# Sandwich block with expert-choice MoE on one core: ranks of the top-k by prefix scans, index lists for two experts at a time, and a later second gather

## The reference

```python
# E = 16, C = int(T * 2.0 / 16) = 1024, D = 256, I = 1024, IS = 512
logits = flat_x @ gate_w.T
scores = softmax(logits, axis=-1).T               # E x T
topk_weight, topk_idx = top_k(scores, C)          # per expert
xg = flat_x[topk_idx]                             # gather
g = einsum('ecd,eid->eci', xg, Wg);  u = einsum('ecd,eid->eci', xg, Wu)
eo = einsum('eci,edi->ecd', gelu(g) * u, Wd) * topk_weight[..., None]
flat_out = zeros.at[topk_idx].add(eo)             # scatter-add
shared = (gelu(hidden @ Sg.T) * (hidden @ Su.T)) @ Sd.T    # every token
x = x + layernorm(flat_out + shared)
```

## Time and profile before

| what | value |
|---|---|
| median of three runs | 2111.92 us |
| profiled execution, its span | 2114.11 us, 2112.3 us |
| TensorE busy | 2030.2 us (96% of the span) |
| TensorE weight load busy | 1814.4 us (86%) |
| VectorE busy | 1195.0 us (57%) |
| ScalarE busy | 971.2 us (46%) |
| GpSimd busy | 436.1 us (21%) |
| granted TensorE clock, mean | 0.981 |

### The profile page before, as it was taken

How to read it: one execution, slowest core, us unless ns; L and a number is a source line. 1 busy time by engine, 2 the same in 40 slices (tenths; PEclk the granted TensorE clock), 3 DMA queues, 4 the chain that set the end, 5 groups by cost and what they waited for, 6 DMA issues and landing times.

```text
span 2112.3 us, 32697 instructions
## 1 busy us (share of the span) xinstructions
PE 2030.2 (96%) x12590; PEld 1814.4 (86%) x12592; DVE 1195.0 (57%) x2518; ACT 971.2 (46%) x1809; POOL 436.1 (21%) x450
## 2 busy tenths in 40 slices
PE   7999999999994998899999999999999999999996
PEld 6899999999984887788888888888989898888885
DVE  5586686677663876555465545444453535343565
ACT  4464564564542334344444444444443434344543
POOL 0000000000001000313323332333233222322255
PEclk8999999999995999999999999999999999999998
DMA  3011110111015111233333333333333333334266
GB/s 112 1 41 42 61 62 41 60 78 43 32 51 196 66 61 41 63 100 74 71 82 79 73 72 82 80 75 75 79 77 79 77 78 91 62 92 100 53 196 131
DMA packets 55556, 159.91 MB, mean 76 GB/s; under 512 B 9472, under 2 KB 25984, under 8 KB 48256
## 3 DMA queue, kind: packets, MB, share of 16 engines
q1 hardware_dynamic: 28912, 116.16, 15.3%
q0 software_dynamic: 26512, 41.96, 12.5%
HBM read 98.78 MB, written 59.31 MB: 75 GB/s over the span
## 4 chain that ended last, share of the span: by engine, by line
PE 64%; DVE 2%; issue 1%; POOL 1%; ACT 1%; DVEq 0%; another core or an unknown queue 0%; ACTq 0%; POOLq 0%
PE mo_psD L58 7%; PE mo_psD L60 7%; PE mo_psD L59 7%; PE mo_psG L58 7%; PE mo_psU L58 7%; PE mo_psG L59 7%; PE mo_psG L60 7%; PE mo_psU L60 7%; PE mo_psU L59 7%; PE mo_psX L1217 1%; PE mo_psX L1033 1%; DVE mo_st L1509 0%; POOL mo_rs L1799 0%; DVE mo_HF L1545 0%; DVE mo_XT_lo L1485 0%
## 5 line engine op out<-in xcount | busy, mean ns | idle before, releaser
L1545 DVE TENSOR_TENSOR mo_HF<-mo_psU,mo_HF 128x512 f32<-128x512 f32 x320 | 221.2, 691 | 645.7 <-ACT mo_HF L1386 625.1
L1386 ACT ACTIVATE mo_HF<-mo_psG 128x512 f32<-128x512 f32 x320 | 191.2, 598 | 478.4 <-PE mo_psU L60 428.9
L1771 POOL DMA_INDIRECT ACC<-mo_OUT,mo_GI x128 | 202.9, 1585 | 700.4 <-ACT mo_OUT L1453 690.9
L60 PE MATMUL mo_psD<-mo_wd_hi,mo_H_lo 128*128 128x256 f32 x1024 | 289.8, 283 | 0.0
L59 PE MATMUL mo_psD<-mo_wd_lo,mo_H_hi 128*128 128x256 f32 x1024 | 289.8, 283 | 0.0
L58 PE MATMUL mo_psD<-mo_wd_hi,mo_H_hi 128*128 128x256 f32 x1024 | 289.6, 283 | 0.0
L1490 DVE TENSOR_TENSOR mo_H_lo<-mo_HF,mo_H_hi 128x512 fp32r<-128x512 f32 x300 | 204.5, 682 | 0.0
L1364 ACT ACTIVATE mo_H_hi<-mo_HF 128x512 fp32r<-128x512 f32 x320 | 199.7, 624 | 1.0 <-DVE mo_HF L1545 1.0
L59 PEld LDWEIGHTS mo_psD<-mo_wd_lo,mo_H_hi 128*128 128x128 f32 x1024 | 196.5, 192 | 1.3
L58 PEld LDWEIGHTS mo_psD<-mo_wd_hi,mo_H_hi 128*128 128x128 f32 x1024 | 196.5, 192 | 1.2
L60 PEld LDWEIGHTS mo_psD<-mo_wd_hi,mo_H_lo 128*128 128x128 f32 x1024 | 196.5, 192 | 0.0
(11 more groups left out here) (262 smaller groups left out, 5177.1 us busy)
## 6 DMA issues: line engine op xcount, KB each, us to landing
X1a<-wg_in SPq DMA_DIRECT2D x16, 1024.0 KB, 4.9
X1a<-wu_in SPq DMA_DIRECT2D x16, 1024.0 KB, 4.9
X1a<-wd_in SPq DMA_DIRECT2D x16, 1024.0 KB, 4.9
XN<-XNB SPq DMA_DIRECT2D x8, 1088.0 KB, 4.1
X<-x_in SPq DMA_DIRECT2D x8, 1024.0 KB, 6.2
out_dram<-X SPq DMA_DIRECT2D x8, 1024.0 KB, 4.3
XN2T<-xn2T SPq DMA_DIRECT2D x8, 1024.0 KB, 3.8
mo_F<-ACC SPq DMA_DIRECT2D x7, 1024.0 KB, 13.0
```

The lines of the kernel that those rows point to most:

```text
L60: return pe.matmul(out, w_lo, x_hi, start=False, stop=last)
L1386: a.activation(HF[:, it % 2, :], psG[:, it % 2, :], ACT.Gelu).then_inc(s_gelu, 1)
L1545: v.tensor_tensor(HF[:, it % 2, :], psU[:, it % 2, :], HF[:, it % 2, :], ALU.mult).then_inc(s_mul, 1)
L1771: g.indirect_dma_start(out=io["ACC"], out_offset=bass.IndirectOffsetOnAxis(ap=GI[n % 2][:, 4 * tb + t:4 * tb + t + 1], axis=0), in_=OUT[:, ...
```

## The change

Three things change.

First, ranks. The masks stay in the transposed layout. A running count along each partition's 1024 columns (`v_scan`, one for each mask) gives every token's place among its partition's marked ones, and three matmuls of one column (`p_off`) with a 0/1 matrix `before` (same expert, earlier partition) and `same` (same expert) give what the other partitions add. VectorE adds, selects and joins the two (`v_slot`, `v_slot2`), TensorE transposes the 128 x 1024 result back by eight matmuls (`p_slot`), and ScalarE copies it as integers (`a_slot`). The 16 transposes, the 20 counting matmuls, their copies and the prefix sums over tables are gone.

Second, lists. `GROUPS, GE` is 8, 2 in place of 4, 4. A group has two chunks of 64 columns, each column holding 32 positions for 2 experts, and the matmuls of a chunk are 32 of 64 x 64 in place of 16 of 128 x 128. There are still 16 chunks: two stand before the experts, at steps 35 and 36, and fourteen in blocks E0+1 to E0+14. SyncE writes and reads lists eight times, with two writes each, in place of four times with four. The list of experts 2 and 3 is decoded in `down(E0+2)`; before, experts 0 to 3 had theirs in the first list.

Third, `gather(1)` waits until TensorE has finished four steps of block E0.

```diff
-GROUPS, GE = 4, 4
+GROUPS, GE = 8, 2
...
+        if x == 28:
+            self.v_scan(v, self.SG, self.GT)
+        if x == 29:
+            self.v_scan(v, self.SE, self.EQ)
         if x == 29.5:
-            self.v_prefix(v)
-            self.v_ahead(v)
-        if x == 31:
-            self.v_rank(v)
             self.v_slot(v)
+        if x == 30:
+            self.v_slot2(v)
         if x == 32:
-            self.v_slot2(v)
             self.v_digits(v)
-        if x == 33:
+        if x == 33.5:
             self.v_lo1(v, 0)
-        if x == 33.5:
             self.v_hival(v, 0)
         if x == 34:
-            self.v_acc(v, 0)
             self.v_lo1(v, 1)
         if x == 35:
+            self.v_acc(v, 0)
             self.v_hival(v, 1)
         if x == 36:
             self.v_acc(v, 1)
...
             self.v_dec(v, 0)
...
-        if x in (34, 36, 37.5, 39):
-            self.p_list(pe, (34, 36, 37.5, 39).index(x))
+        if x == 29.5:
+            self.p_off(pe)
+        if x == 31:
+            self.p_slot(pe)
+        if x in (35, 36):
+            self.p_list(pe, x - 35)
...
+        if x == 31:
+            self.a_slot(a)
         if x == 33:
             self.a_digits(a)
...
+    def v_scan(self, v, out, mask):
+
+        v.tensor_tensor_scan(out[:, :], mask[:, :], mask[:, :], 0.0, ALU.add, ALU.max).then_inc(self.s_scan, 1)
+
+    def p_off(self, pe):
+
+        pe.wait_ge(self.s_scan, 2)
+        gt, eq = (t[:, SC_N - 1:SC_N] for t in (self.SG, self.SE))
+        pe.matmul(self.ps[:, 0, 0:1], self.before[:, :], gt, start=True, stop=True)
+        pe.matmul(self.ps[:, 0, 1:2], self.before[:, :], eq, start=True, stop=False)
+        pe.matmul(self.ps[:, 0, 1:2], self.same[:, :], gt, start=False, stop=True).then_inc(self.s_off, 1)
+
+    def v_slot(self, v):
+
+        v.wait_ge(self.s_off, 1)
+        v.tensor_scalar(self.OFF[:, :], self.ps[:, 0, 0:2], -4097.0, None, ALU.add)
         v.drain()
+        v.scalar_tensor_tensor(self.SG[:, :], self.SG[:, :], self.OFF[:, 0:1], self.GT[:, :], ALU.add, ALU.mult)
+        v.scalar_tensor_tensor(self.SE[:, :], self.SE[:, :], self.OFF[:, 1:2], self.EQ[:, :], ALU.add, ALU.mult)
         v.drain()
+    def v_slot2(self, v):
+        v.scalar_tensor_tensor(self.SLOT[:, :], self.SG[:, :], 4096.0, self.SE[:, :], ALU.add, ALU.add).then_inc(self.s_slot, 1)
+
+    def p_slot(self, pe):
+        pe.wait_ge(self.s_slot, 1)
+        for t in range(8):
+            i = pe.transpose(self.ps[:, t // 4, t % 4 * P:(t % 4 + 1) * P], self.SLOT[:, t * P:(t + 1) * P], self.c.ident[:, :])
+        i.then_inc(self.s_slt, 1)
...
-            i = pe.matmul(self.ps[:, 0, 0:SL * GE], self.lo1[:, t, :, :].rearrange("p v e -> p (v e)"),
+            i = pe.matmul(self.ps[0:SL * GE, 0, 0:SL * GE], self.lo1[:, t, :, :].rearrange("p v e -> p (v e)"),
                           self.val[:, :, t * GE:(t + 1) * GE], start=(t == 0), stop=(t == tiles - 1))
...
-                if n in (2, 4, 6):
-                    topk.store(sp, n // 2)
+                if 1 <= n < GROUPS:
+                    topk.store(sp, n)
...
                 wait(g, s_tw, n - 1)
+                if n == 1:
+                    wait(g, s_up, base[E0] + 4)
```

More of the change, by code:

```diff
@@ L725, in __init__ @@
         self.hi1, self.val = new("hi1", [P, SL, CW], BF16), new("val", [P, SL, CW], BF16)
-        self.vf = new("vf", [P, GE * SL])
-        self.vu, self.vj, self.vp = (new(n, [P, GE * SL], I32) for n in ("vu", "vj", "vp"))
-        self.LS = new("LS", [P, GROUPS, GE, SL], I32)
+        self.vf = new("vf", [GE * SL, GE * SL])
+        self.vu, self.vj, self.vp = (new(n, [GE * SL, GE * SL], I32) for n in ("vu", "vj", "vp"))
+        self.LS = new("LS", [GE * SL, GROUPS, GE, SL], I32)
         self.zero = mem.over("zero", [P, 4 * D], F32, "lo1", 0)
@@ L841, in pool @@
         g.iota(self.TVi[:, :], [[P * NU, 4], [P, NU], [0, GE]], base=P * P, channel_multiplier=1)
-        g.memset(self.ones[:, :], 1.0)
         for i in range(NBIT + 4):
@@ L901, in v_const @@
         v.tensor_scalar(self.same[:, :], self.mcolf[:, :], self.mrowf[:, 0:1], None, ALU.is_equal)
+        v.drain()
+        v.tensor_tensor(self.before[:, :], self.before[:, :], self.same[:, :], ALU.mult)
         v.wait_ge(self.s_scv, 1)
@@ L906, in v_masks @@
         thr = self.cand[:, 0:1].bitcast(F32)
[L907 to L931, removed]
-            i = pe.matmul(self.ps[:, 0, :], self.ones[:, :], self.mk(j), start=(j == 0), stop=(j == 3))
-        i.then_inc(self.s_tot, 1)
@@ L935, in a_tot @@
-    def a_tot(self, a):
-        a.wait_ge(self.s_tot, 1)
-        a.activation(self.tot[0][:, :, :, :].rearrange("p k u e -> p (k u e)"), self.ps[:, 0, :], ACT.Copy).then_inc(self.s_totc, 1)
-    def p_rank(self, pe, js):
-        for j in js:
-            pe.wait_ge(self.s_totc, 1)
-            if j >= 1:
-                wait(pe, self.s_rkc, j - 1)
-            for jj in range(4):
-                i = pe.matmul(self.ps[:, (j + 1) % 2, :], (self.incl if jj < j else self.strict)[:, :], self.mk(jj),
-                              start=(jj == 0), stop=(jj == 3))
-            i.then_inc(self.s_rank, 1)
@@ L980, in v_slot @@
-    def v_slot(self, v):
-        for k in range(2):
-            v.scalar_tensor_tensor(self.RK[:, :, k, :], self.RK[:, :, k, :], -4096.0, self.MK[:, :, k, :], ALU.add, ALU.mult)
+        v.tensor_scalar(self.GT[:, :], self.SCT[:, :], thr, None, ALU.is_gt)
+        v.tensor_scalar(self.EQ[:, :], self.SCT[:, :], thr, None, ALU.is_equal)
+        v.drain()
+    def v_scan(self, v, out, mask):
+        v.tensor_tensor_scan(out[:, :], mask[:, :], mask[:, :], 0.0, ALU.add, ALU.max).then_inc(self.s_scan, 1)
@@ new lines, in p_slot, with a_slot @@
+    def p_slot(self, pe):
[3 more added lines that the diff above has]
+        i.then_inc(self.s_slt, 1)
+    def a_slot(self, a):
+        a.wait_ge(self.s_slt, 1)
+        for h in range(2):
+            i = a.activation(self.SI[:, :].rearrange("p (j n) -> p j n", j=4)[:, :, h * P:(h + 1) * P],
+                             self.ps[:, h, :].rearrange("p (j q) -> p j q", j=4), ACT.Copy)
+        i.then_inc(self.s_si, 1)
```

91 lines of the change are left out of this document (17 added, 74 removed).

## The result

The changed kernel takes 2120.26 us (median of 6 runs, 2118.32 to 2123.04), the kernel before 2112.56 us (6 runs). The ratio is 1.0042, with a 95% interval of 1.0028 to 1.0056: slower by 0.42%, where I forecast 2111 us and no more than 2119. The profiled execution took 2122.61 us, its span is 2120.8 us against 2112.3.

What follows compares the result with a forecast made beforehand. TensorE, busy 96% of the span, was taken as the bound. Terms -3.7 - 7.7 - 0.6 - 6.0 + 3.2 + 14.1 = -0.7 us took 2114.1 to 2113.4; the median, 2.2 lower, gave 2111 us, range 2096 to 2119.

Steps and rivals of the forecast that it cites:

- Ranks, matmuls and waits: Rank stage before the experts: matmuls save 3.7 us; TensorE's waits and half clock, less new waits, save 7.7 us.
- Second gather: Delayed gather(1): ScalarE's stop, TensorE's 4.3 us wait and 1.7 us of half clock go, -6.0 us.
- The other end: Second gather's other bound: 0 us saved, if ScalarE's stop has another cause.
- First list: Two chunks at steps 35 and 36: +0.7 us waiting for tables, -1.3 us at step 43's transposes, sum -0.6 us.
- List of experts 2 and 3: Block E0+3: TensorE waits 3.2 us for gathered rows, bounds 2.5 and 4; 1.7 us more if the clock falls.
- Lists' matmuls: All 16 list chunks: 32 small matmuls at 56 ns each, +0.88 us a chunk, +14.1 us in all.
- the bound of 57: Upper bound for one 64 x 64 list matmul: 57 ns, as much as the nearest one in the trace.
- VectorE's tables: List tables on VectorE: inner runs shrink from 4 to 2, costed at nothing.
- the fast pairs: Rival on list matmuls: 64-column pairs run by their columns, lists cost as before, sum -14.8, 2097 us; chance 28%.
- the in-between ones: Rival on list matmuls: pairs take 40 ns, sum -8.9 us, time 2103 us; chance 8%.
- the third rival: First gather comes no earlier, SyncE holding the list behind block 8's store; transposes' 1.3 us stay, 2112 us; no separate chance.
- The stop of ScalarE: Rival: the stop comes again in E0 or before; 6.0 us stay, 2117 us, decides from 48 ns pairs; chance 14%.

Runs made afterwards that it cites:

- E0: Not a run: the block where the experts start; from the last threshold product to its first transposes, 113.5 us in the kernel before, 98.1 in the changed kernel.
- Scans only: The changed kernel with lists of four experts again and the second gather back right behind the first, so the new ranks alone: 2102.4 us, ratio 0.9948 to the kernel before.
- four: The changed kernel with lists of four experts put back; ranks by scans and the delayed second gather stay: 2095.7 us, ratio 0.9922 to the kernel before.
- nowait: The changed kernel with the second chunk's matmuls one step later and each list decoded ahead of the next chunk's tables: 2113.0 us, ratio 1.0002 to the kernel before.
- pairs16: The changed kernel with two tiles in each list matmul, 16 of 128 x 128 a chunk, diagonal blocks added on VectorE: 2104.5 us, ratio 0.9958 to the kernel before.
- pad128: The changed kernel with 128 weight columns in every list matmul, the extra output rows unused: 2115.0 us, ratio 1.0018 to the kernel before.

## Why the prediction was wrong

The place was named and the sign wrong. By its own steps:

- **Ranks, matmuls and waits, -3.7 and -7.7: right.** Scans only shows -10.8 us in the stage for -11.4. The scan takes 2.28 us for 2.3, the new waits 1.1, 0.6 and 0.4 for 1.2, 0.6 and 0.5. A small slip in it: half of the 5.38 us of work at half clock is 2.7 us, not 2.5.
- **Second gather, -6.0: right.** -6.7 alone, -7.3 on top of the scans (scans only against four). The other end, 0, is excluded.
- **First list, -0.6: wrong.** The chunk's tables made TensorE wait 2.9 us for 2.4, and the clock then fell: 4.0 us of product work at half clock, 2 us more than at full. The sum has nothing for that; the forecast named the fall only among what would show it wrong. By the earlier trace rows the clock had fallen behind 4.3 us and not behind 1.7; a wait of 2.4 lay between, and I priced the end that was kinder. The transposes' 1.3 us went as forecast.
- **List of experts 2 and 3, +3.2: the wait right, its follow-up missing.** The wait was 3.1 us. The half clock behind it cost another 2.8 (counted from the last threshold product, the lead over before shrinks from 9.8 us at 1002.87 to 7.0 at 1008.89), which stood only in the bounds, as 1.7.
- **Lists' matmuls, +14.1: mis-sized.** Measured +1.18 us a chunk for 0.88, 18.9 us for 14.1. The cost of one small matmul was right, 56 ns inside the chunk for the 56 taken, and so was the bound of 57. What failed is that a chunk was taken as its matmuls and nothing else. Its edges cost 0.08 us before and 0.36 now; they are the 0.3 us missing in each chunk.
- **VectorE's tables, 0: wrong.** The `lo` table went from 1.22 to 2.08 us. VectorE has no idle time from the second chunk's `lo` table at 833.22 to the end of its `mo_val` at 838.9, nor from 985.26 to the decode of the list in E0+3, so up to 0.9 us of each of the two long waits is that table. No run takes it out alone.

The sum of the missing parts: clock and longer wait at the second chunk 2.7 us in E0 (15.4 ahead for the 18.1 that the terms make), half clock in E0+3 2.8, chunks behind E0 18.5 for 14.1, 4.4. With 0.1 less for the wait in E0+3 that is 9.8 on a forecast of -0.7, 9.1 as the stage shows. The span's 8.5 has 0.6 us more ahead of the stage and 1.3 less behind it; in the changed kernel a wait of 2.3 us there has no half clock behind it, in the kernel before it has (last section).

Of the rivals, the fast pairs and the in-between ones fell (57 ns is no 28 or 40). The first gather did come forward, at 858.1 for 873.8, and its wait of 1.3 us went, so the third rival fell too. The stop of ScalarE did not come in the changed kernel as a long wait. (That rival's 48 ns is 46 by the sum's own terms.) The slower side that happened was none of them: it was the forecast's own terms, two with a half clock behind them that was left out, and one without its edges. The range had room for a fallen clock only on top of that rival, and ended 1.3 us short.

## What to carry to other kernels

A short matmul that brings its own weights cost 57 ns here at 64 moving columns, whether it had 64 or 128 bf16 weight columns, and no more at 128 x 128. So a cut that halves the tile and doubles the number doubled the cost, and two tiles side by side with a diagonal result gave it back. Price such a group twice: by the distance of two starts inside it, and by the difference of two periods with and without it, since it also pays at its edges, and pays more there with narrow weights. When a change puts a wait of 2 us or more on TensorE, give the half clock behind it a term and a chance of its own: here it cost up to 2.8 us behind a wait of 3.1, and once nothing behind one of 3.2. And split a change of three parts before judging it: two of these gave 17 us, the third took 25.

## What the runs showed of the hardware that was not expected

- List matmuls of 64 x 64, 128 x 64 and 128 x 128 (weight by moving columns, bf16) follow each other at 56 to 57 ns, those of 64 x 128 at 73. A chunk of them costs 0.1 us more at its edges with 128 weight columns, and 0.3 to 0.4 with 64.
- The length of a wait of TensorE alone does not tell whether the clock falls. It stood at half behind waits of 4.8, 4.3, 3.5, 3.1, 2.9, 2.7 and of 1.8 us (nowait, pairs16), and not behind those of 1.7 us ahead of a list chunk. But in pairs16 the wait of 3.2 us in E0+3 has full clock behind it, where that of 3.1 us in the changed kernel has half; and the same wait of 2.3 us near the end has half clock behind it in the kernel before and full clock in the changed one. What decides stays open. Pairs16, then the kernel before, then the changed kernel:

```profile
1001.53 0.66 PE L1158 MATMUL mo_psX<-ident,mo_XG 128*128 128x128 f32 x4 [3.18 <-DMA mo_XG<-XN,mo_GI]
1001.50:1004.50 3.00, 2.96 (x15) 2.55 (x16) 0.69 (x1) 0.60 (x1) 2.39 (x3) 1.00 0.89 276
```

```profile
2062.16 0.58 PE L58 MATMUL mo_psD<-mo_wg_hi,mo_H_hi 128*128 128x256 f32 x1 [2.30 <-DVE mo_F L1517]
2062.20:2065.20 3.00, 3.00 (x14) 3.00 (x15) 1.25 (x4) 2.20 (x5) 2.51 (x8) 0.50 0.12 23
```

```profile
2071.99 0.39 PE L58 MATMUL mo_psD<-mo_wg_hi,mo_H_hi 128*128 128x256 f32 x1 [2.31 <-DVE mo_F L1451]
2072.00:2075.00 3.00, 3.00 (x25) 3.00 (x26) 2.03 (x5) 2.23 (x5) 2.51 (x8) 1.00 0.20 38
```

- At half clock (0.50 from 839 to 841) the 32 matmuls of 64 x 64 took no longer than at full, 1.98 us by the row at 839.04, while 16 of 128 x 128 took 1.86 us for 1.07:

```profile
839.04 1.98 PE L967 MATMUL mo_psX<-mo_val,mo_lo 128*64 128x64 bf16 x32 [2.94 <-DVE mo_val L957]
```

```profile
837.53 1.86 PE L969 MATMUL mo_psX<-mo_val,mo_lo 128*128 128x128 bf16 x16 [3.54 <-DVE mo_val L957]
```

- A comparison over 2048 bf16 elements took 1.22 us when its innermost run was 4 elements long and 2.08 us when it was 2.
- ScalarE stopped for 3.2 to 5.3 us beside series of indirect DMAs in five kernels here (before, scans only, nowait, pad128, pairs16) and the profile names no cause that accounts for it.
